# Second projection: query and key tiles turned in 32x32 blocks by VectorE, heads scaled out of PSUM by ScalarE, eight banks for tiles

## The reference, cut to what matters

```python
q = einsum('bsd,ed->bse', x, Wq).reshape(bsz, seqlen, HQ, D)     # HQ = 32, D = 128
k = einsum('bsd,ed->bse', x, Wk).reshape(bsz, seqlen, HK, D)     # HK = 8
v = einsum('bsd,ed->bse', x, Wv).reshape(bsz, seqlen, HK, D)
q, k = rmsnorm(q, q_norm_w), rmsnorm(k, k_norm_w)                # over d, head by head
q, k = rope(q, pos), rope(k, pos)                                # two halves of d, cos and sin
scores = einsum('bqhd,bkhd->bhqk', q, k_all) * SCALE             # sums over d
```

## Time and profile before

| | |
|---|---|
| runs | 1645.44, 1645.83, 1647.90 us; median 1645.83 |
| profiled execution | 1646.35 us, its span 1644.5 us |
| busy in the span | PE 1598.2 us (97%), DVE 1099.2 (67%), ACT 944.3 (57%), POOL 321.4 (20%) |
| this stage | 548.6 to 848.2 us: PE 298.99 us of 299.60 busy, DVE 209.75, ACT 188.53, POOL 162.50 |

### The profile page before, as it was taken

The page is one execution under the profiler, slowest core; times in us unless marked ns, Lnnn a source line. Parts: engine busy times, 40 slices in busy tenths (PEclk is TensorE's granted clock), DMA queues, the critical chain, the costliest instruction groups (busy, mean ns, idle before and its releaser), DMA issues. The chain is left out here.

```text
span 1644.5 us, 33852 instructions
## 1 busy us (share of the span) xinstructions
PE 1598.2 (97%) x10728; PEld 1394.2 (85%) x10728; DVE 1099.2 (67%) x2907; ACT 944.3 (57%) x2398; POOL 321.4 (20%) x327
## 2 busy tenths in 40 slices
PE   3999999999999999999999999999999999999998
PEld 3887888888888788888879999999999999977777
DVE  7305543554346777777748999999999999764443
ACT  4224323232322376676758999999999999722221
POOL 2200000000000165665611112112111211022210
PEclk9999999999999999999999999999999999999999
DMA  6531122201210334344568999999999999595401
GB/s 217 189 135 59 61 71 70 70 5 65 70 64 27 126 95 133 110 134 133 186 220 286 313 312 300 322 310 296 321 313 307 305 318 311 175 309 153 126 2 51
DMA packets 230099, 290.74 MB, mean 177 GB/s; under 512 B 17658, under 2 KB 181914, under 8 KB 221850
## 3 DMA queue, kind: packets, MB, share of 16 engines
q1 hardware_dynamic: 220250, 222.83, 43.1%
q0 software_dynamic: 9216, 67.11, 11.5%
q10 hardware_dynamic: 576, 0.07, 0.0%
HBM read 237.44 MB, written 50.41 MB: 175 GB/s over the span
## 5 line engine op out<-in xcount | busy, mean ns | idle before, releaser
L1636 PE MATMUL p_val<-probs_t,vals 128*128 128x128 f32 x2048 | 271.3, 275 | 0.0
L1636 PEld LDWEIGHTS p_val<-probs_t,vals 128*128 128x128 f32 x2048 | 248.6, 192 | 0.1
L1545 DVE CUSTOM_DVE_ANT_0 probs<-p_score,mask 128x544 f32<-128x544 f32 x256 | 184.4, 720 | 41.9 <-issue 34.8
L1449 ACT ACTIVATE probs<-probs,low 128x544 f32<-128x544 f32 x256 | 190.1, 743 | 0.7 <-DVE low L1545 0.6
L1534 DVE TENSOR_TENSOR wo_lo<-keys,wo_hi 128x544 fp32r<-128x544 f32 x224 | 161.8, 722 | 0.2 <-ACT wo_hi L1444 0.2
L477 PE MATMUL p_tile<-w_hi,y_hi 128*128 128x512 f32 x384 | 157.1, 409 | 2.4 <-PEq L490 2.4
L1457 ACT ACTIVATE probs_t<-p_turn 128x512 f32<-128x512 f32 x256 | 149.0, 582 | 16.9 <-PE p_turn L1615 16.8
L1120 POOL TENSOR_TENSOR w_lo<-w_raw,w_hi 128x512 fp32r<-128x512 f32 x44 | 57.3, 1304 | 507.0 <-DVE w_hi L1155 489.0
L1615 PE MATMUL p_turn<-cst,probs 128*128 128x128 f32 x1024 | 153.6, 272 | 0.7 <-ACT probs_t L1457 0.7
L1444 ACT ACTIVATE wo_hi<-keys 128x544 fp32r<-128x544 f32 x224 | 145.6, 650 | 14.3 <-PE p_score L479 14.1
L477 PE MATMUL p_score<-wo_hi,q_hi 128*128 128x272 f32 x448 | 149.3, 333 | 2.4 <-DVE low L1545 1.2
(11 more groups left out here) (219 smaller groups left out, 3550.1 us busy)
## 6 DMA issues: line engine op xcount, KB each, us to landing
keys<-in_k_pages SPq DMA_DIRECT2D x512, 128.0 KB
qk_new<-x_res SPq DMA_DIRECT2D x80, 256.0 KB, 2.2
x_res<-qk_new SPq DMA_DIRECT2D x32, 512.0 KB
o_new<-x_res SPq DMA_DIRECT2D x32, 512.0 KB, 6.5
w_raw<-in_w_vkq_t SPq DMA_DIRECT2D x12, 1024.0 KB, 5.6
w_raw<-in_w_qkv_t SPq DMA_DIRECT2D x10, 1024.0 KB, 8.5
toep<-kpad SPq DMA_DIRECT2D x32, 256.0 KB, 4.3
w_raw<-in_w_dense_t SPq DMA_DIRECT2D x8, 1024.0 KB, 5.5
```

Of the source, the lines that this page charges most:

```text
L1449: nc.scalar.activation(probs[:, i % 8, :], probs[:, i % 8, :], ACT.Exp, bias=low[:, i % 4:i % 4 + 1], scale=-1.0, accum_out=total[:, i % 4 ...
L1545: v.tensor_tensor_reduce(out=probs[:, i % 8, :], in0=score_at(i % 2, slice(0, KEYS)), in1=mask[:, i // HK, :], scale=1.0, scalar=3e38, op0 ...
L1636: mm = pe.matmul(p_val[:, h, half * P:(half + 1) * P], vals[slot][:, c // RUN, c % RUN * HK * D + k * D:c % RUN * HK * D + (k + 1) * D], p ...
```

## The change

PE no longer transposes. The tile takes this way (lines of the changed file in brackets):

- PE makes tile i into one of 8 banks (before: 4, and two for `p_turn`).
- ACT squares heads 0 to 2 in one instruction without sums and head 3 with its sum (L1085, L1086); in the next iteration takes the root (L1091); one later scales the 4 heads out of PSUM into `part_a` in SBUF (L1099). That frees the bank. `put` is gone.
- DVE sums the squares of heads 0 to 2 (L1193), one iteration later inverts (L1197), three later forms two products of the whole tile with the tables, `part_b` (L1205) and `part_a` in place (L1206), five later turns 32x32 blocks of the added tile into `stage` (L1215).
- POOL adds the products into `joined` (two buffers), written so that 32-wide blocks of the 4 heads stand together (L1143). It waits for the products (`parts_ready`) and, for the buffer, for the turn of the tile two before (`staged`).
- d comes out in the order block by block; the DMA stores it so, and the cached keys are laid out alike on the host.
- The first weight pieces are split by ACT, not DVE. SP issues weight loads at `i % 8 == 1` (before 5), and at the end a value store ahead of a turned tile's behind the other.

```diff
-        p_tile = ctx.enter_context(nc.psum_tensor("p_tile", [P, 4, E], F32))
-        p_turn = ctx.enter_context(nc.psum_tensor("p_turn", [P, 2, 4, P], F32))
+        p_tile = ctx.enter_context(nc.psum_tensor("p_tile", [P, 8, E], F32))
...
-                late = [TT - LAG + i // 2 if i % 2 == 0 else TT + i // 2 for i in range(2 * LAG)]
+                late = [TT + i // 2 if i % 2 == 0 else TT - LAG + i // 2 for i in range(2 * LAG)]
...
-                    if i % TT == EC + 1 and not last:
+                    if i % TT == 1 and not last:
...
-                    sp.dma_start(qk[b0:b0 + 4, :, bass.ds(to[i // TT], P)].rearrange("b d n -> d b n"),
-                                 stage[:, i % 4, :, :, :].rearrange("d b h s -> d b (h s)")).then_inc(stored[i % 4], 16)
+                    sp.dma_start(qk[b0:b0 + 4, :, bass.ds(to[i // TT], P)].rearrange("b (d j) n -> (b d) j n", j=4),
+                                 stage[:, i % 4, :].rearrange("p (j n) -> p j n", j=4)).then_inc(stored[i % 4], 16)
...
+            def square(m, i):
+                act.wait_ge(tile_done, m * PAIR + i + 1)
+                nc.scalar.activation(squared[:, i % 2, 3, :], p_tile[:, i % 8, 3 * D:4 * D], ACT.Square, accum_out=squares[:, i % 4, 3:4])
+                nc.scalar.activation(squared[:, i % 2, 0:3, :].rearrange("p h d -> p (h d)"), p_tile[:, i % 8, 0:3 * D],
+                                     ACT.Square).then_inc(squares_ready, 1)
...
+                for h in range(4):
+                    ins = nc.scalar.activation(part_a[:, i % 4, h, :], p_tile[:, i % 8, h * D:(h + 1) * D], ACT.Copy,
+                                               scale=inv_rms[:, i % 4, h:h + 1])
+                ins.then_inc(tile_taken, 1)
...
-                pool.wait_ge(tile_taken, m * PAIR + i + 1)
-                nc.gpsimd.tensor_tensor(part_a[:, i % 4, :, :], part_a[:, i % 4, :, :], part_b[:, i % 4, :, :],
-                                        ALU.add).then_inc(rotated, 1)
+                u = m * PAIR + i - TT
+                pool.wait_ge(parts_ready, u + 1)
+                if not (isinstance(u, int) and u < 2):
+                    pool.wait_ge(staged, u - 1)
+                blocks = lambda a: a.rearrange("p h (j c) -> p h j c", j=4)
+                nc.gpsimd.tensor_tensor(joined[:, i % 2, :].rearrange("p (j h c) -> p h j c", j=4, h=4), blocks(part_a[:, i % 4, :, :]),
+                                        blocks(part_b[:, i % 4, :, :]), ALU.add).then_inc(rotated, 1)
...
+                v.wait_ge(tile_taken, m * PAIR + i + 1)
+                v.tensor_tensor(halves(part_b[:, i % 4, :, :])[:, :, ::-1, :], halves(scaled), halves(tables_of(1)), ALU.mult)
+                v.tensor_tensor(scaled, scaled, tables_of(0), ALU.mult).then_inc(parts_ready, 1)
...
+                v.wait_ge(rotated, u + 1)
+                if not (isinstance(u, int) and u < 4):
+                    v.wait_ge(stored[i % 4], 4 * (u - i % 4))
...
+                v.transpose(out=stage[:, i % 4, :], in_=joined[:, i % 2, :]).then_inc(staged, 1)
...
+                    for what, lag in ((add_squares, 0), (invert, 1), (rotate, 3), (turn, 5)):
+                        tile = turned_tile(m, i - lag, first, last)
+                        if tile:
+                            what(*tile)
...
-                    pe.wait_ge(tile_taken, t - 3)
+                if not (isinstance(t, int) and t < 8):
+                    pe.wait_ge(tile_taken, t - 7)
...
-            def turn(m, i):
...
-                for h in range(4):
-                    mm = pe.transpose(p_turn[:, i % 2, h, :], part_a[:, i % 4, h, :], ident)
-                mm.then_inc(turned, 1)
```

More of the change, by code:

```diff
@@ L998, in cached_qkv @@
         squares_ready = sem("squares_ready")
+        sums_ready = sem("sums_ready")
         rms_ready = sem("rms_ready")
         inv_ready = sem("inv_ready")
+        parts_ready = sem("parts_ready")
         rotated = sem("rotated")
-        turned = sem("turned3")
         staged = sem("staged")
@@ L1015, in cached_qkv, with turned_tile @@
         values = lambda i, first, last: first and i < TT or last and i >= TT
+        def turned_tile(m, i, first, last):
+            if i < 0:
+                return None if first else (m - 1, PAIR + i)
+            return None if values(i, first, last) else (m, i)
         block = ctx.enter_context(nc.Block())
@@ L1063, in _, with take_values @@
         def _(act):
-            def take_values(w, i):
-                if w == TT:
-                    act.wait_ge(tile_taken, TT + TURNED)
+            def take_values(m, w, i):
+                act.wait_ge(tile_done, m * PAIR + i + 1)
                 if w >= 2:
                     act.wait_ge(v_stored[i % 2], 16 * (w // 2))
-                nc.scalar.activation(v_out[:, i % 2, :], p_tile[:, i % 4, :], ACT.Copy).then_inc(tile_taken, 1)
+                nc.scalar.activation(v_out[:, i % 2, :], p_tile[:, i % 8, :], ACT.Copy).then_inc(tile_taken, 1)
             def split_hi(n, slot, c):
-                if c == 0:
+                if c == 0 and not (isinstance(n, int) and n == 1):
                     act.wait_ge(w_in[slot], 8 * (n - slot))
@@ L1076, in split_hi, with root, scale @@
                 nc.scalar.activation(w_hi[:, slot, c, :], w_raw[:, slot, c, :], ACT.Copy).then_inc(hi_piece, 1)
-            def put(m, i):
+            def square(m, i):
+                act.wait_ge(tile_done, m * PAIR + i + 1)
+                nc.scalar.activation(squared[:, i % 2, 3, :], p_tile[:, i % 8, 3 * D:4 * D], ACT.Square, accum_out=squares[:, i % 4, 3:4])
+                nc.scalar.activation(squared[:, i % 2, 0:3, :].rearrange("p h d -> p (h d)"), p_tile[:, i % 8, 0:3 * D],
+                                     ACT.Square).then_inc(squares_ready, 1)
+            def root(m, i):
+                act.wait_ge(sums_ready, m * PAIR + i - TT + 1)
+                nc.scalar.activation(rms[:, i % 4, :], squares[:, i % 4, :], ACT.Sqrt, bias=eps[:, :], scale=1.0 / D).then_inc(rms_ready, 1)
+            def scale(m, i):
                 u = m * PAIR + i - TT
-                act.wait_ge(turned, u + 1)
+                act.wait_ge(inv_ready, u + 1)
                 if not (isinstance(u, int) and u < 4):
[L1082 to L1086, removed]
+                    act.wait_ge(rotated, u - 3)
+                for h in range(4):
+                    ins = nc.scalar.activation(part_a[:, i % 4, h, :], p_tile[:, i % 8, h * D:(h + 1) * D], ACT.Copy,
+                                               scale=inv_rms[:, i % 4, h:h + 1])
+                ins.then_inc(tile_taken, 1)
             def body(m, first, last):
@@ L1092, in body @@
                         nc.scalar.activation(ang[:, :, :, :], ang[:, :, :, :], ACT.Sin).then_inc(sines3, 1)
[L1093 to L1098, removed]
-                    for h in range(4):
[L1101 to L1110, removed]
+                    if not values(i, first, last):
+                        square(m, i)
+                    tile = turned_tile(m, i - 1, first, last)
+                    if tile:
+                        root(*tile)
+                    tile = turned_tile(m, i - 2, first, last)
+                    if tile:
+                        scale(*tile)
+                    elif i >= 2:
+                        take_values(m, i - 2, i - 2)
+                    if 1 <= i % TT <= EC and not (last and i >= TT):
                         split_hi(2 * m + 1 + i // TT, (1 + i // TT) % 2, i % TT - 1)
             pairs(body, act)
+            for i in range(PAIR - 2, PAIR):
+                take_values(PAIRS - 1, i, i)
         @block.gpsimd
@@ L1126, in rotate @@
             def rotate(m, i):
-                pool.wait_ge(tile_taken, m * PAIR + i + 1)
-                nc.gpsimd.tensor_tensor(part_a[:, i % 4, :, :], part_a[:, i % 4, :, :], part_b[:, i % 4, :, :],
-                                        ALU.add).then_inc(rotated, 1)
+                u = m * PAIR + i - TT
[5 more added lines that the diff above has]
+                                        blocks(part_b[:, i % 4, :, :]), ALU.add).then_inc(rotated, 1)
             def tiles(m, first, last):
                 for i in range(PAIR):
[L1134 to L1137, removed]
+                    tile = turned_tile(m, i - 4, first, last)
+                    if tile:
+                        rotate(*tile)
                     if 1 <= i % TT <= EC and not values(i, first, last):
@@ L1178, in _, with add_squares, invert @@
                 step(v.tensor_scalar(rot[:, which, 1, :, D // 2:D], rot[:, which, 1, :, D // 2:D], -1.0, None, ALU.mult))
-            def scale_and_rotate(m, i, key):
+            def add_squares(m, i):
+                v.wait_ge(squares_ready, m * PAIR + i - TT + 1)
+                v.tensor_reduce(squares[:, i % 4, 0:3], squared[:, i % 2, 0:3, :], X, ALU.add).then_inc(sums_ready, 1)
+            def invert(m, i):
+                v.wait_ge(rms_ready, m * PAIR + i - TT + 1)
```

(34 more changed lines are left out.)

8 lines of the change are left out of this document (3 added, 5 removed).

## The result

The changed kernel takes 1688.10 us (median of 4 runs, 1687.57 to 1688.46), the kernel before, on the same chip, 1646.87 us (1645.44 to 1648.08): a ratio of 1.0251, 95% interval 1.0237 to 1.0265. The change is slower by 41 us. The profiled execution took 1688.17 us with a span of 1686.3 us, 41.8 more than before. Forecast: 1681, range 1652 to 1712.

What follows compares the result with a forecast made beforehand. DVE, colliding with POOL over SBUF, was taken to bound the changed stage in place of PE. The stage's terms summed to 334.2 us against 299.6, so 1646.35 + 34.6 = 1681 us, range 1652 to 1712.

Steps and rivals of the forecast that it cites:

- What bounds: In the changed stage, DVE with POOL sets the pace: tiles of 3.15 or 4.25 us, above PE's 2.72.
- The two holds: With SBUF operands, a POOL operation of 1.29 us holds off DVE for 1.15; a DVE product holds off POOL for 0.55.
- Whoever waits is next: DVE and POOL alternate when they collide, so a waiting POOL operation gets in between two DVE instructions.
- Periods: Time per turned tile on DVE: 3.15 us without a weight piece, 4.25 us with one.
- The 74 periods: From tile 8's products to tile 82's, 37 periods of 4.25 and 37 of 3.15 us: 273.8 us.
- The piece gets between the products: POOL's weight subtraction runs between DVE's two products and holds the second: 1.10 us more per tile with a piece.
- the rival in which they stay together: The piece runs beside the turn instead; period with a piece 3.55 us, total 1655 us; chance 0.08.
- POOL waits for the turn: POOL's add waits for the turn of the tile two before (buffer `joined`), starting 0.09 us after DVE's end.
- Costing nothing: Splitting first weights on ACT, same-size stores and weight loads four tiles earlier add no time; ACT's work stays below DVE's.
- the 334.2 forecast: End of the changed stage, counted in us from PE's first matmul, against 299.6 before: 34.6 us more.
- the clock: PE's clock drops after idling, before the last chunk of values: worth 0 to 1.7 us, taken as 1.
- The tail: Value copies and stores end up to 6 us after PE because SP holds value stores behind turned tiles; 6 taken.

Runs made afterwards that it cites:

- the run with the heads in PSUM: Changed kernel, but ScalarE writes the scaled heads back into their PSUM bank, where both VectorE products read them: 1611.40 us, ratio 0.979 to the kernel before.
- the two runs that take this wait out of the way: Changed kernel with four buffers of `joined` instead of two (1642.58 us); changed kernel with VectorE's turn ordered before the two products (1639.96 us).
- with four buffers: Changed kernel with four buffers of `joined` instead of two, so POOL's add waits for an older turn: 1642.58 us, ratio 0.998 to the kernel before.
- without pieces: Changed kernel without GpSimd's weight subtractions after the first chunk, so the output is not the reference's: 1646.83 us in a single execution.
- with VectorE's scaling: Changed kernel without ScalarE's scaling; VectorE multiplies head, 1/rms and table out of PSUM in eight instructions a tile: 1645.40 us, ratio 0.9995 to the kernel before.
- with the turn ahead: Changed kernel with VectorE's turn ordered before the two products, two buffers of `joined` kept: 1639.96 us, ratio 0.9962 to the kernel before.

## Why the prediction held, point by point

- *What bounds.* "DVE, with POOL, sets the pace": shown by the windows and by the run with the heads in PSUM, where the collision goes and PE has 218.00 of 218.00 us.
- *The two holds.* A POOL operation holds a DVE product to about 0.15 us before its end, 1.15 of 1.29, as the earlier trace rows had it. The Trainium skill, SBUF — State Buffer, section "Who interferes with whom", has such a pair block for the whole instruction. The trace agrees on the blocking and on who takes part (products with one operand in PSUM, the sum and the turn were not held), but not on the length: by whole lengths periods would have been 3.29 and 4.67; 3.20 and 4.28 were measured. "Whoever waits is next" is too strong: it held in the tiles that set the pace and failed once (843.01). It cost nothing there: the two periods around it were 2.33 and 5.19 us, together as long as 3.20 and 4.31.
- *Periods.* Forecast 3.15 and 4.25, measured 3.20 and 4.28: POOL starts 0.15, not 0.09, behind the turn. The 74 periods took 275.3 us (585.73 to 861.03) against 273.8.
- *The piece gets between the products.* Shown, 1.1 us each; the rival in which they stay together falls.
- *POOL waits for the turn.* Shown by the two runs that take this wait out of the way: 45 and 48 us less.
- *Costing nothing.* ACT waited for DVE 108 us; POOL's add with runs of 32 columns kept 1.29; PE did not wait for the first weights.
- *The size.* The stage's end came 6.3 us later behind PE's first matmul (549.68) than the 334.2 forecast, and that matmul itself 1.1 later than before; in the other runs here it came at 548.5 to 550.9, so the 1.1 can't be put down to the change. Of the 6.3, 2.0 lie ahead of tile 8's products, 1.5 in the periods, 0.9 in the last piece, 1.2 in the last chunk of matmuls and 0.7 in the tail, all one way, so that the sum did not come near by errors that cancel. The term mis-sized is the clock, taken as 1 us once: the last chunk took 24.0 us for 21.8, so 2.2 there, and about 1.7 more were lost at the start. On this path the clock fell twice: 0.58 in the first 4 us, behind an idle time of 2.44, and 0.50 in 4.1 us behind one of 6.32 (1.2 GHz, the lower level, for most of the first and all of the second). It fell at the chunks between as well (0.92 in the middle window), but there DVE sets the pace. The first can't be put down to the change: behind the same 2.44 us the clock stayed at 1.00 in the profiled executions of the kernel before, with four buffers, with the heads in PSUM and with four banks; it fell in those without pieces, with VectorE's scaling and with the turn ahead.
- *The tail.* 6.7 us from PE's last matmul, forecast 6, but partly for another reason, so that the nearness is in part luck. Timeline of ACT and of SP's queue:

```profile
871.52 1.10 ACT L1075 ACTIVATE v_out<-p_tile 128x512 f32<-128x512 f32 x2
882.65 0.60 ACT L1075 ACTIVATE v_out<-p_tile 128x512 f32<-128x512 f32 x1 [10.04 <-DMA v_new<-v_out]
...
863.30 9.64 SPq L926 DMA_DIRECT2D keys<-in_k_pages  x16
872.99 2.69 SPq L1053 DMA_DIRECT2D qk_new<-x_res  x4
877.63 0.62 SPq L1035 DMA_DIRECT2D v_new<-v_out  x1
```

ACT had two value tiles copied by 872.62, but SP was issuing loads of cached keys until 872.94, and the store that frees the first copy's buffer came at 877.63 and landed some 5 us later, not 2.1. I had put the lateness down to the turned tiles ahead of it in SP's order alone.

Not tried: a version in which the weight pieces leave POOL while all products read SBUF, and products of which only one reads PSUM.

## What to carry to other kernels

Before moving work off TensorE, ask where the operands of the work that replaces it lie: here two VectorE products cost 0.66 and 0.68 us with one operand in PSUM and up to 1.78 with both in SBUF (once 3.53) while GpSimd worked, which made 77 us between two versions with the same instructions but for where ScalarE writes (1688 and 1611 us). Two operands in SBUF are not the only case: the casts of the earlier trace rows read one tensor, from SBUF, and two of the four took 1.52 us beside POOL where the shortest took 0.42. If a collision can't be taken away, the order of the instructions decides how much of it counts: what does not collide (a turn, a sum) should run beside the other engine's operation, so that the wait in front of that operation must not be for the last thing ahead of the colliding one. A change of several parts must be looked at as a whole: the turn on VectorE and eight banks gave nothing without ScalarE's scaling (1645.40 us), cost 41 us with the scaling into SBUF, and gained 35 with the scaling in PSUM; with four banks that version took 1967.98. Eight banks or the scaling without the turn were not run.

## What the runs showed that I had not expected

ScalarE can scale a tile in place in PSUM at the price of a copy to SBUF (0.353 against 0.363 us for 128 columns), while PE writes other banks. And behind idle times of the same 2.44 us PE's matmuls took 0.63 us at first in four of the eight profiled executions and 0.39 in the four others, so that a difference of some 2 us at such a place tells nothing of an edit.
